# Expert weights loaded one stage earlier, and an expert stage that works on pairs of batches and four experts at a time

## The reference, cut to what matters

```
t  = t + y_scan @ W_out * silu(z) ...            # x2, per batch [1024 tokens, 64]
n  = layernorm(t)                                # "normed"
logits = n @ gate_w.T + gate_b                   # [batch, 1024, 32 experts]
probs  = softmax over the 1024 tokens
vals, idx = top 8 tokens of each expert
pooled[b, e] = sum over the 8 of vals * n[idx]   # 64 values
h   = gelu([pooled, 1] @ weight1[e])             # [65] x [65, 256]
out = [h, 1] @ weight2[e]                        # [257] x [257, 64]
result[b, idx] += vals * out                     # scattered back to the tokens
final = t + result
```

## Time and profile before

| | us |
|---|---|
| median of 3 runs | 6785.05 |
| fastest and slowest of them | 6782.85, 18169.33 |
| span of the profiled execution | 6778.7 |
| gate stage, first load landed to last store | about 6476 to 6611 |
| expert stage | 6611.6 to 6778.7 |

### The profile page before, as it was taken

How to read it: one execution, slowest core, us unless ns; L and a number is a source line. 1 busy time by engine, 2 the same in 40 slices (tenths; PEclk the granted TensorE clock), 3 DMA queues, 4 the chain that set the end, 5 groups by cost and what they waited for, 6 DMA issues and landing times. The chain is left out here.

```text
span 6778.7 us, 154979 instructions
## 1 busy us (share of the span) xinstructions
PE 6279.5 (93%) x52177; PEld 3795.6 (56%) x52177; DVE 6198.5 (91%) x3824; ACT 4532.8 (67%) x9559; POOL 2334.7 (34%) x6840
## 2 busy tenths in 40 slices
PE   8999989999969999999999999999999999999867
PEld 3567843333236666666666666666666666666535
DVE  7888878888849999999999999999999999999972
ACT  7888858888736666666666666666666666666641
POOL 5555545555423232332323323323233232332210
PEclk9999999999979999999999999999999999999995
DMA  6666666666622121121212212212122121221164
GB/s 143 155 154 154 155 145 153 156 153 156 153 68 54 39 63 47 48 54 47 55 47 48 56 44 58 50 42 59 47 52 51 42 59 47 51 49 42 27 187 115
DMA packets 929532, 563.47 MB, mean 83 GB/s; under 512 B 697101, under 2 KB 834221, under 8 KB 928941
## 3 DMA queue, kind: packets, MB, share of 16 engines
q1 hardware_dynamic: 928957, 556.40, 34.6%
HBM read 159.23 MB, written 124.13 MB: 42 GB/s over the span
## 5 line engine op out<-in xcount | busy, mean ns | idle before, releaser
L1029 DVE TENSOR_TENSOR_SCAN states<-decay,enter_ps 128x1024 f32<-128x1024 f32 x2048 | 4465.4, 2262 | 75.4 <-PE enter_ps L732 66.0
L857 ACT ACTIVATE decay<-rate_ps 128x512 f32<-128x512 f32 (+1 forms) x4096 | 2221.2, 594 | 338.0 <-PE rate_ps L718 146.0
L732 PE MATMUL enter_ps<-s_steps,s_tokens 128*128 128x128 bf16 x16384 | 2142.2, 310 | 293.5 <-DVE states L1029 284.1
L732 PEld LDWEIGHTS enter_ps<-s_steps,s_tokens 128*128 128x128 bf16 x16384 | 1596.5, 129 | 1415.3 <-DVE states L1029 1167.2
L718 PE MATMUL rate_ps<-s_wide,s_decays 128*128 128x256 bf16 x8192 | 1318.4, 283 | 14.2 <-ACT decay L857 7.6
L964 POOL TENSOR_TENSOR product<-decay,states 128x16 f32<-128x16 f32 x1920 | 462.2, 241 | 2195.2 <-ACT decay L857 2191.7
L243 POOL TENSOR_TENSOR entered<-gates 128x512 f32<-128x512 f32 x512 | 899.9, 1758 | 888.7 <-ACT gates L203 888.7
L864 ACT COPY enter_ps<-at_first 128x16 f32<-128x16 f32 x1920 | 338.1, 176 | 1223.9 <-PE enter_ps L732 1186.2
L760 PE MATMUL y_ps<-states,spread 128*32 128x512 f32 x8192 | 1090.3, 604 | 2.4 <-issue 2.4
L718 PEld LDWEIGHTS rate_ps<-s_wide,s_decays 128*128 128x128 bf16 x8192 | 904.3, 118 | 74.7 <-ACT decay L857 19.7
L161 PE MATMUL pre<-rows,weights_left 128*32 128x512 f32 x8192 | 905.4, 595 | 36.0 <-POOL rows L236 23.8
(11 more groups left out here) (135 smaller groups left out, 2473.3 us busy)
## 6 DMA issues: line engine op xcount, KB each, us to landing
rows<-feat SPq DMA_DIRECT2D x1024, 132.0 KB, 2.4
rows<-feat SPq DMA_DIRECT2D x512, 128.0 KB, 2.4
s_steps<-steps_dram SPq DMA_DIRECT2D x4096, 8.0 KB
rows<-feat SPq DMA_DIRECT2D x512, 127.8 KB, 2.4
s_wide<-rates_dram SPq DMA_DIRECT2D x1024, 32.0 KB, 1.9
s_tokens<-tokens_dram SPq DMA_DIRECT2D x2048, 16.0 KB, 2.0
rates_dram<-parts SPq DMA_DIRECT2D x64, 384.0 KB, 3.3
steps_dram<-parts SPq DMA_DIRECT2D x64, 384.0 KB, 3.4
```

The lines of the kernel that those rows point to most:

```text
L732: mm = pe.matmul(out.rearrange("p h l -> p l h"), tokens[s][:, k, :], steps[s][:, k, :, d:d + half], start=True, stop=True)
L857: act.activation(decay[i][:, half, at:], rate_ps[h][:, :, at:], ACT.Exp).then_inc(decay_ready, 1)
L1029: dve.tensor_tensor_scan(out, factor, term, 0.0, ALU.mult, ALU.add).then_inc(scanned, 1)
```

## The change

The expert weights get tiles that live through the gate and the expert stage. In the gate stage ScalarE now issues their loads: the bias at the start, and in each of the 16 turns two experts of w1 and two of w2, just behind `deviation`. w2 is laid out so that two neighbouring hidden units of an expert are one run in memory (512 bytes where it was 256).

In the expert stage every quad of logits and every pair of batches of tokens has its own buffer, so no load waits for anything. Tokens come as pairs of batches on 128 partitions. One transpose handles both batches of a pair, and one row of eight matmuls pools both (the two blocks of the output that mix the batches are not used). The first layer has `pooled` stationary (32 columns, of which 16 are batches and 16 are zero) and 256 columns of w1 moving, four experts beside each other in the four column groups of the array. Its output has batches on partitions, so `hidden` is transposed (16 transposes, new, with four VectorE copies, new). The second layer runs four experts beside each other too. The results leave in four stores where there was one.

```diff
-    build_gate(nc, y, z_dram, x1_dram, w_out, mean_w, identity, gate_w, gate_b, x2_dram, normed_dram, logit_dram)
+    held["gate"] = dict(y_dram=y, z_dram=z_dram, x1_dram=x1_dram, w_out=w_out, mean_w=mean_w, gate_w=gate_w,
+                        gate_b=gate_b)
...
+def expert_phase(nc, logit_dram, normed_dram, x2_dram, identity, weight1, weight2, expert_dram, out_dram):
+    with ExitStack() as ctx:
+        w1 = ctx.enter_context(nc.sbuf_tensor("w1", [CH + 1, EXPERTS, HIDDEN], F32))
+        w2 = ctx.enter_context(nc.sbuf_tensor("w2", [128, EXPERTS, HIDDEN // 128, CH], F32))
+        w2_bias = ctx.enter_context(nc.sbuf_tensor("w2_bias", [1, EXPERTS, CH], F32))
+        weights_in = ctx.enter_context(nc.semaphore("expert_weights_in"))
+        build_gate(nc, identity=identity, x2_dram=x2_dram, normed_dram=normed_dram, logit_dram=logit_dram,
+                   w1=w1, w2=w2, w2_bias=w2_bias, weight1=weight1, weight2=weight2, experts_in=weights_in, **held["gate"])
+        build_experts(nc, logit_dram, normed_dram, x2_dram, identity, w1, w2, w2_bias, weights_in, expert_dram, out_dram)
...
-            pipelined(act, (0, gate_values), (3, add_bias), (1, deviation))
+            act.dma_start(w2_bias[:, :, :], weight2[:, HIDDEN:HIDDEN + 1, :].rearrange("e h o -> h e o")
+                          ).then_inc(experts_in, DMA)
+
+            def load_experts(b, i, turn):
+                mine = slice(EXPERTS // BATCH * b, EXPERTS // BATCH * (b + 1))
+                act.dma_start(w1[:, mine, :], weight1[mine, :, :].rearrange("e d h -> d e h")).then_inc(experts_in, DMA)
+                act.dma_start(w2[:, mine, :, :].rearrange("p e h o -> p e (h o)"), weight2[mine, 0:HIDDEN, :].rearrange(
+                    "e (p h) o -> p e (h o)", h=HIDDEN // 128)).then_inc(experts_in, DMA)
+
+            pipelined(act, (0, gate_values), (3, add_bias), (1, deviation), (1, load_experts))
...
+            load_logits(0)
             sp.dma_start(ident[:, :], identity).then_inc(consts_in, DMA)
-
...
-            load_logits(0)
             load_logits(1)
             load_tokens(0)
             load_tokens(1)
-            sp.dma_start(w1[:, :, :], weight1.rearrange("e d h -> d e h")).then_inc(weights_in, DMA)
-            for h in range(2):
-                sp.dma_start(w2[:, h, :, :], weight2[:, 128 * h:128 * h + 128, :].rearrange("e h o -> h e o")
-                             ).then_inc(weights_in, DMA)
-            sp.dma_start(w2_bias[:, :, :], weight2[:, HIDDEN:HIDDEN + 1, :].rearrange("e h o -> h e o")
-                         ).then_inc(weights_in, DMA)
...
+            for q in range(2, QUADS):
+                load_logits(q)
+                load_tokens(2 * q - 2)
+                load_tokens(2 * q - 1)
+            for j in range(2 * QUADS - 2, DUOS):
+                load_tokens(j)
             for j in range(DUOS):
                 sp.dma_start(x2[j][:, :], x2_dram[2 * j:2 * j + 2, :, :].rearrange("b c l -> (b c) l")).then_inc(x2_in, DMA)
-            sp.wait_ge(results_ready, 4)
-            sp.dma_start(expert_dram, results[:, :, :]).then_inc(results_out, DMA)
-            sp.wait_ge(results_out, DMA)
+            sp.wait_ge(results_ready, 1)
+            for j in range(LANES):
+                dst = expert_dram.rearrange("b (m j) o -> j b m o", j=LANES)[j, :, :, :]
+                sp.dma_start(dst, results[ROW * j:ROW * j + BATCH, :, :]).then_inc(results_out, DMA)
+            sp.wait_ge(results_out, LANES * DMA)
...
+            def turn_tokens(j):
+                pe.wait_ge(normed_in[j], DMA)
+                for h in range(2):
+                    if j:
+                        pe.wait_ge(normed_t_ready, 2 * j - 1 + h)
+                    for t in range(4):
+                        at = 128 * (4 * h + t)
+                        mm = pe.transpose(normed_ps[h][:, 128 * t:128 * t + 128], normed[j][:, at:at + 128], ident[:, :])
+                    mm.then_inc(normed_turned, 1)
+
+            def pool_tokens(j):
+                q, first = 2 * j // GROUP, 2 * j % GROUP
+                pe.wait_ge(chosen_t_ready, 2 * (q + 1))
+                pe.wait_ge(normed_t_ready, 2 * (j + 1))
+                if j >= 2:
+                    pe.wait_ge(pooled_ready, j - 1)
                 for t in range(TILES):
-                    mm = pe.transpose(turned_ps[b % 2][:, t, :], normed[b % 2][:, 128 * t:128 * t + 128], ident[0:CH, 0:CH])
-                mm.then_inc(normed_turned, 1)
+                    mm = pe.matmul(pooled_ps[j % 2][:, 0:2 * EXPERTS], normed_t[j % 2][:, t, :],
+                                   chosen_t[q % 2][:, t, EXPERTS * first:EXPERTS * first + 2 * EXPERTS],
+                                   start=(t == 0), stop=(t == TILES - 1))
+                mm.then_inc(pooled_summed, 1)
...
-            pe.wait_ge(weights_in, 4 * DMA)
+                for h in range(2):
+                    if q:
+                        pe.wait_ge(chosen_t_ready, 2 * q - 1 + h)
+                    for t in range(4):
+                        at = 128 * (4 * h + t)
+                        mm = pe.transpose(chosen_ps[h][:, 128 * t:128 * t + 128], chosen[q][:, at:at + 128], ident[:, :])
+                    mm.then_inc(chosen_turned, 1)
+                turn_tokens(2 * q + 1)
+                pool_tokens(2 * q)
+                if q + 1 < QUADS:
+                    turn_tokens(2 * q + 2)
+                pool_tokens(2 * q + 1)
+            pe.wait_ge(weights_in, (1 + 2 * BATCH) * DMA)
             pe.wait_ge(ones_set, 2)
-            pe.wait_ge(pooled_ready, BATCH)
...
+            def first_layer(k):
+                for m in (2 * k, 2 * k + 1):
+                    for j in range(LANES):
+                        e, at = LANES * m + j, HIDDEN * (m % 2)
+                        mm = pe.matmul(hidden_ps[k][ROW * j:ROW * j + ROW, at:at + HIDDEN], pooled[:, e, :],
+                                       w1[:, e, :], start=True, stop=True)
+                mm.then_inc(hidden_summed, 1)
+
+            def turn_hidden(k):
+                pe.wait_ge(hidden_ready, k + 1)
+                for m in (2 * k, 2 * k + 1):
+                    for h in range(HALVES):
+                        at = 128 * (m % 2 * HALVES + h)
+                        mm = pe.transpose(hidden_t_ps[k][:, at:at + 128], hidden[:, m, h::HALVES], ident[:, :])
+                mm.then_inc(hidden_turned, 1)
+
+            def second_layer(k):
+                pe.wait_ge(hidden_t_ready, k + 1)
+                for m in (2 * k, 2 * k + 1):
+                    for h in range(HALVES + 1):
+                        for j in range(LANES):
+                            e = LANES * m + j
+                            out = results_ps[ROW * j:ROW * j + ROW, CH * m:CH * m + CH]
+                            if h < HALVES:
+                                mm = pe.matmul(out, hidden_t[:, m, h, ROW * j:ROW * j + ROW], w2[:, e, h, :],
+                                               start=(h == 0), stop=False)
+                            else:
+                                mm = pe.matmul(out, ones[:, :], w2_bias[:, e, :], start=False, stop=True)
+                return mm
+
+            for k in range(4):
+                first_layer(k)
+            turn_hidden(0)
+            turn_hidden(1)
+            second_layer(0)
+            turn_hidden(2)
+            second_layer(1)
+            turn_hidden(3)
+            second_layer(2)
+            second_layer(3).then_inc(results_summed, 1)
...
+            for k in range(4):
+                dve.wait_ge(hidden_turned, k + 1)
+                dve.tensor_copy(hidden_t[:, 2 * k:2 * k + 2, :, :].rearrange("p m h b -> p (m h b)"),
+                                hidden_t_ps[k][:, :]).then_inc(hidden_t_ready, 1)
+            dve.wait_ge(results_summed, 1)
+            dve.tensor_copy(results[:, :, :].rearrange("p m o -> p (m o)"), results_ps[:, :]).then_inc(results_ready, 1)
...
+            def move_pooled(j):
+                dve.wait_ge(pooled_summed, j + 1)
+                for i in range(2):
+                    p = dve.tensor_copy(pooled[0:CH, :, 2 * j + i],
+                                        pooled_ps[j % 2][CH * i:CH * i + CH, EXPERTS * i:EXPERTS * i + EXPERTS])
+                p.then_inc(pooled_ready, 1)
```

More of the change, by code:

```diff
@@ L1249, in expert_phase @@
     DUOS = BATCH // 2
+    ROW = 32
+    LANES = 128 // ROW
+    TURNS = EXPERTS // LANES
+    HALVES = HIDDEN // 128
     with ExitStack() as ctx:
@@ L1268, in expert_phase @@
         share = sb("share", [128, QUADS])
[L1269 to L1274, removed]
+        chosen_t = [sb(f"chosen_t{i}", [128, TILES, 128]) for i in range(2)]
+        normed = [sb(f"e_normed{j}", [2 * CH, LEN]) for j in range(DUOS)]
+        normed_t = [sb(f"normed_t{i}", [128, TILES, 2 * CH]) for i in range(2)]
+        pooled = sb("pooled", [ROWS1, EXPERTS, ROW])
+        hidden = sb("hidden", [128, TURNS, HIDDEN])
+        hidden_t = sb("hidden_t", [128, TURNS, HALVES, 128])
+        results = sb("results", [128, TURNS, CH])
```

(32 more changed lines are left out.)

117 lines of the change are left out of this document (31 added, 86 removed).

## The result

The changed kernel takes 6698.91 us (median; 6697.44 to 6701.0, 4 runs) against 6785.24 before: a ratio of 0.9875, 95% interval 0.9861 to 0.989. That is 86 us, 1.3% faster. The forecast was 6743, range 6712 to 6764: right on "faster by less than 2%", but the gain is twice the forecast and outside its range. Run once more beside later variants, the same kernel took 6700.44 (6699.7 to 6704.07), ratio 0.9878 [0.9861, 0.9894].

What follows compares the result with a forecast made beforehand. Expert stage taken as one serial chain, TensorE waiting for tokens, then busy at clock 0.50. 21.1 + 21.1 + 8.1 - 1.3 = 49.0 saved, less 7 in the gate stage, 42.0: 6743 us, range 6712 to 6764.

Steps and rivals of the forecast that it cites:

- TensorE's clock in the pooling: Expert stage, pooling: clock stays at 0.50, 51.3 us plus 0.3 for the second pooled copy; saves 21.1.
- The rival: Pooling: clock rises to 1.0, so pooling takes 29 us instead of 51 and the kernel 6721; chance 15%.
- 6755 with half of the other: Range's upper end, 6764: second layer not side by side (6755, 13%) or weights paid in full (6756, 10%), plus half the other.
- Second layer, its price per pass: Expert stage, second layer: 192 passes at 0.08 us, 15.4; sum 20.2 against 28.3, saves 8.1 (-4 to 17).
- The lower bound I had: Second layer: columns alone, 0.033 us a 64-column pass at half clock, 6.3 us in all.
- the first layer: Expert stage: 64 passes of 256 columns in four column groups take 6.4 us; saves 21.1 of 27.5.
- The layers' clock: Expert stage: first layer starts at the low level, 6.4 us taken between 4.2 and 8.5; second layer priced near half clock.
- Gate stage: ScalarE's two weight issues a turn, between g_std and swish's table load, add 0.47 us a turn; costs 7.
- the term that I put at nothing: Gate stage: weight transfers make loads land later, 0 to 1.3 us a turn, 0 to 20 in all; nothing taken.
- its full price, 20 us: Gate stage rival: loads pay for the weights in full, 1.3 us a turn, 20 instead of 7, kernel 6756; chance 10%.
- The wait for tokens: Expert stage, pooling: TensorE waits 14.01 us for tokens behind w2's issue; its removal is nearly all of pooling's 21.1 saved.
- the small terms: Expert stage: up to the transposes of chosen 0, results out and back costs 1.3, scatter and last store 0.

Runs made afterwards that it cites:

- the run with the early issue: Changed kernel with ScalarE's two weight issues moved from between g_std and the table load of swish to right behind swish; 6705.24 us, ratio 0.9882.
- pairs undone: Changed kernel with each batch's tokens transposed and pooled by themselves on TensorE, the rest as changed; 6719.06 us, ratio 0.9893.
- the rebuild alone: Changed kernel, but SyncE loads the expert weights in the expert stage, behind the tokens, with nothing added to the gate stage; 6697.1 us, ratio 0.9871.
- the pause: Changed kernel, but TensorE waits for ScalarE's copies of chosen before it transposes tokens, about 0.7 us a quad; 6712.98 us, ratio 0.9898.
- single transposes: Changed kernel with only the token transposes undone to single batches, pooling still on pairs; 6719.01 us, ratio 0.9908.

## Why the prediction was wrong

1. *TensorE's clock in the pooling: the step that failed.* I wrote that TensorE was 92% busy for 51 us and the clock stayed at 0.50, so the new work would stay there too. The row was right and the inference was not: what TensorE did mattered, not how busy it was. Pooling took 28.1 us where the sum had 51.6: 23.6 us of the 41 missed. About 19 of them are the clock. That is an estimate: at the low level 4 + 7 rows of transposes at 1.91 and 8 rows of passes at 3.31 (the run with the early issue, before its clock rose; forecast 3.43) are 47.5. The other 4 are waits of 0.7 a quad that did not come and the slightly lower price. The rival had the mechanism (128-column transposes of chosen and tokens in one row) and the price (29 us of pooling), but I gave it 15%, and it took the clock only to the end of pooling: its 6721, and the 6712 at the low end of the range, left the layers at the low level. The upper end has a small error too: 6755 with half of the other is 6762, not 6764.

2. *Second layer, its price per pass: mis-sized.* Forecast 0.08; at the low level 0.040 (24 passes in 0.95 us, pairs undone), at the high one 0.025. The lower bound I had (0.033) was near the truth; the 0.08 was chosen from the stationary side of single matmuls, and no row showed short passes in groups. With the first layer at 7.05 (forecast 6.4), both layers at the low level take 18.8 us where I had 26.6: 7.8 us.

3. *The layers' clock.* I let the first layer rise from low to high and put the second at the low level. In the changed kernel the clock came raised and both layers ran at 1.0: 11.45 us instead of 18.8 at the low level, 7.4 us. It is no fixed property of the layers: with pairs undone they stayed at 0.50 throughout, and in two profiles (the rebuild alone, and the pause) the clock fell in the first layer and rose again in the second, the other way round from what I forecast. Why is open.

4. *Gate stage.* Forecast -7, measured -4.8, and between 0 and -6 in other profiles. The number is near by luck, since the term was the wrong one. The issues do run beside g_std, but what is left of them, 0.17 a turn and not 0.47, does not lengthen the turns (7.61 against 7.60). What costs is late loads, the term that I put at nothing: one turn of 10.8 us is 3.2 of the 4.8. The rule of the Trainium skill, "DMA: Bandwidth & Descriptors", section "Issuing engines are not separate DMA queues", that a second issuer shares the same 16 engines, holds here: moved beside the loads, the pieces delay them (TensorE's waits for loads 14.3 us instead of 8.7). But its full price, 20 us, was not paid. That the pieces mostly fell where the engines were draining would explain it, and is not shown.

5. *The two sides of the change.* The wait for tokens went in both halves of it, so I counted it once, rightly, and never asked which half was needed. The rebuild alone does, within the noise.

The remaining 2.7 us are the gate stage's 2.2 and a scan that ended 1.0 earlier, less 0.5 of the small terms.

## What to carry to other kernels

Before costing a stage at the clock that its old rows show, ask whether the new work differs in kind (wider moving side, fewer and larger steps, no pauses), and price it and all that follows it at both levels: here that was about 27 of the 41 us missed. A raised clock can also be lost: here by small steps with waits between, but also in the layers, with TensorE busy throughout. Loads that no one waits for yet belong behind those that someone does, in the same queue; with the rebuilt stage that was worth as much as moving them a stage earlier. Put short matmuls in an order in which neighbours use different column groups.

## What was not expected of the hardware

Transposes alone raised the clock. TensorE's timeline of the changed kernel has nothing else between 6623.7 and the rise:

```profile
6623.70 1.94 PE L1375 MATMUL e_bank<-e_ident,e_normed 128*128 128x128 f32 x8 [11.77 <-DMA e_normed<-normed_dram]
...
6628.46 1.97 PE L1398 MATMUL e_bank<-e_ident,chosen 128*128 128x128 f32 x8 [2.82 <-DVE chosen L1521]
...
6630.22 1.56 PE L1375 MATMUL e_bank<-e_ident,e_normed 128*128 128x128 f32 x8
```

The Trainium skill, "TensorE: Matmul & The Clock Gate", Part 4, says that the clock does not rise for transposes. This trace does not agree: 0.50 up to 6631, 0.86 in the next microsecond, 1.0 after it. A finer window places the rise:

```profile
6630.40:6631.40 1.00, 1.00 (x7) 1.00 (x6) 0.96 (x3) 0.67 (x2) 0.00 (x0) 0.56 1.02 418
```

0.56 is the low level up to about 6631.3, and the first pooling pass begins at 6631.62. In the rebuild alone the rise, at about 6626.5, also came ahead of the first pooling pass (6626.85).

And one kernel can have two times: with pairs undone 6699 or 6719, with single transposes 6703 to 6729, by whether and when the clock rises. One of four runs was at the other time in the first case, so three runs can miss it.
